# Attention layer with fp32-exact projections: ScalarE empties projection banks at the head of a unit, VectorE takes the softmax weight behind the score copy

## The reference

```python
def proj(w, b):
    return (x_seq @ w + b).reshape(B, S, NUM_HEADS, d_k).transpose(0, 2, 1, 3)
q, k, v = proj(wq, bq), proj(wk, bk), proj(wv, bv)
scores = jnp.einsum('bhqd,bhkd->bhqk', q, k) / jnp.sqrt(jnp.float32(d_k))
scores = scores + _spatial_bias_matrix(spatial_bias, H, W)[None, None]
attn = jax.nn.softmax(scores, axis=-1)
ctx = jnp.einsum('bhqk,bhkd->bhqd', attn, v).transpose(0, 2, 1, 3).reshape(B, S, d_model)
resid = ctx @ wo + bo + x_seq
out = (resid - mu) * jax.lax.rsqrt(var + LN_EPS) * ln_gamma + ln_beta
```

## Time and profile before

| | us |
|---|---|
| median of 3 runs | 4246.48 (4232.23 to 4246.49) |
| profiled execution | 4250.4 |
| its span, first to last instruction | 4248.5 |
| PE busy | 3415.7 (80%) |
| ACT busy | 2790.0 (66%) |
| DVE busy | 2606.1 (61%) |
| POOL busy | 1182.9 (28%) |
| granted PE clock, mean | 0.900 |

### The profile page before, as it was taken

How to read it: one execution, slowest core, us unless ns; L and a number is a source line. 1 busy time by engine, 2 the same in 40 slices (tenths; PEclk the granted TensorE clock), 3 DMA queues, 4 the chain that set the end, 5 groups by cost and what they waited for, 6 DMA issues and landing times. The chain is left out here.

```text
span 4248.5 us, 138744 instructions
## 1 busy us (share of the span) xinstructions
PE 3415.7 (80%) x52744; PEld 2233.4 (53%) x52744; DVE 2606.1 (61%) x5941; ACT 2790.0 (66%) x7015; POOL 1182.9 (28%) x2824
## 2 busy tenths in 40 slices
PE   4788788887888778888787887878888798877886
PEld 3455455554555455555555554545555555555554
DVE  2566666566666656656566565656656566666665
ACT  2676676766766667676666766667666676766764
POOL 0004214041240412315133150421404124041335
PEclk8899899898998989899898998989999899898988
DMA  4222222223222222312222222232222322222220
GB/s 136 54 62 59 70 64 65 56 61 75 57 64 56 69 61 59 78 46 67 65 57 72 54 60 65 57 76 57 66 55 63 73 57 65 55 68 67 58 64 19
DMA packets 318064, 269.31 MB, mean 63 GB/s; under 512 B 109883, under 2 KB 240955, under 8 KB 317271
## 3 DMA queue, kind: packets, MB, share of 16 engines
q10 hardware_dynamic: 145120, 129.00, 12.8%
q1 hardware_dynamic: 172152, 130.19, 12.1%
HBM read 193.73 MB, written 63.53 MB: 61 GB/s over the span
## 5 line engine op out<-in xcount | busy, mean ns | idle before, releaser
L791 ACT ACTIVATE prob<-prob,own 128x450 f32<-128x450 f32 x1920 | 1269.8, 663 | 1119.0 <-DVE own L922 1087.3
L922 DVE CUSTOM_DVE_ANT_0 prob<-s_ps,window 128x450 f32<-128x450 f32 x1920 | 1126.2, 624 | 694.1 <-PE s_ps L673 616.1
L807 ACT ACTIVATE prob<-prob,weight 128x450 f32<-128x450 f32 x1920 | 1169.6, 657 | 3.9 <-DVE weight L931 3.9
L941 DVE STREAM_TRANSPOSE prob_t<-prob 128x960 f32<-128x960 f32 x960 | 1126.2, 1173 | 52.8 <-ACT prob L807 31.9
L673 PE MATMUL s_ps<-k_sb,q_sb 64*32 64x450 f32 x15360 | 974.3, 613 | 177.6 <-DVE own L922 123.3
L588 PE MATMUL r_ps<-xt,w_sb 128*128 128x450 f32 x3072 | 771.1, 397 | 244.4 <-ACT q_sb L747 148.3
L693 PEld LDWEIGHTS pv_ps<-prob_t,values 64*64 64x64 f32 x30720 | 775.0, 137 | 245.4 <-issue 245.3
L693 PE MATMUL pv_ps<-prob_t,values 64*64 64x120 f32 x30720 | 830.3, 263 | 8.2 <-DVE prob_t L941 3.0
L588 PEld LDWEIGHTS r_ps<-xt,w_sb 128*128 128x128 f32 x3072 | 583.8, 199 | 425.1 <-ACT q_sb L747 155.1
L673 PEld LDWEIGHTS s_ps<-k_sb,q_sb 64*32 64x32 f32 x15360 | 245.8, 114 | 639.8 <-issue 637.9
L607 PE MATMUL r_ps<-wv_sb,xt 128*120 128x512 f32 (+1 forms) x1536 | 425.6, 429 | 181.6 <-DVE xt L906 109.9
(11 more groups left out here) (57 smaller groups left out, 1690.3 us busy)
## 6 DMA issues: line engine op xcount, KB each, us to landing
w_sb<-w_split ACTq DMA_DIRECT2D x126, 512.0 KB, 3.9
values<-v_dram ACTq DMA_DIRECT2D x256, 240.0 KB, 4.9
tokens<-in_x SPq DMA_DIRECT2D x214, 240.0 KB, 3.2
other<-own SPq DMA_DIRECT2D x1920, 1.0 KB, 1.7
out<-tokens SPq DMA_DIRECT2D x105, 240.0 KB, 2.7
v_dram<-stage SPq DMA_DIRECT2D x96, 240.0 KB, 2.6
v_dram<-stage SPq DMA_DIRECT2D x32, 180.0 KB, 2.1
tokens<-in_x SPq DMA_DIRECT2D x30, 120.0 KB, 2.4
```

The source lines that it names most:

```text
L791: nc.scalar.activation(prob[:, u % RING, head, 0:HALF], prob[:, u % RING, head, 0:HALF], ACT.Exp, scale=-1.0, bias=own[:, s, 0, c:c + 1], ...
L807: nc.scalar.activation(prob[:, u % RING, head, 0:HALF], prob[:, u % RING, head, 0:HALF], ACT.Copy, scale=weight[:, s, c:c + 1]).then_inc(p ...
L922: nc.vector.tensor_tensor_reduce(prob[:, u % RING, head, 0:HALF], s_ps[:, u % 2, head, 0:HALF], window[:, w0:w0 + HALF // GRID, :].rearran ...
L941: nc.vector.transpose(out=prob_t[:, g % 2, v % PER_GROUP, :, :].rearrange("p h k -> p (h k)"), in_=prob[:, u % RING, :, :].rearrange("p h ...
```

## The change

It is made in two of the five instruction streams, and moves instructions without adding or removing any. In ACT's `body` the loop over `im.evicted(u)` goes from the end of the unit to its head, ahead of the exponentials, the ratios, `normalise`, the loads of values and `keep_context`; the DMA that `keep_piece` issues goes with it. The units of `EVICT` stay, and so does the order of the evictions among each other. The evictions of the prologue (u < 0) keep their place. In DVE's `body`, `weights(u+2)` goes from ahead of `biased_scores(u+6)` to behind it. `PV_STEPS, FULL_STEPS` stay 2 and 8.

```diff
             def body(im, u):
+                for work in im.evicted(u):
+                    if work[0] == "xt":
+                        xt_hi(im, work[1])
+                    elif work[0] == "piece":
+                        keep_piece(im, *work[1:])
+                    elif work[0] == "value":
+                        stage_value(im, work[1])
                 if im.live(u + AHEAD):
                     exponentials(im, u + AHEAD)
                 if u % 2 and im.live(u + 3):
...
                 g = group_at(u - 1)
                 if g is not None:
                     keep_context(im, g)
-                for work in im.evicted(u):
-                    if work[0] == "xt":
-                        xt_hi(im, work[1])
-                    elif work[0] == "piece":
-                        keep_piece(im, *work[1:])
-                    elif work[0] == "value":
-                        stage_value(im, work[1])
 
             images(act, body)
...
             def body(im, u):
                 if im.live(u):
                     turn(im, u)
+                if im.live(u + AHEAD):
+                    biased_scores(im, u + AHEAD)
                 if u % 2 == 0 and im.live(u + 2):
                     weights(im, u + 2)
-                if im.live(u + AHEAD):
-                    biased_scores(im, u + AHEAD)
```

## The result

| | before | after |
|---|---|---|
| median, us | 4239.35 (4 runs, 4230.32 to 4246.49) | 3753.62 (4 runs, 3747.85 to 3760.88) |
| ratio | | 0.8856, 95% interval 0.8828 to 0.8884 |
| span of the profiled execution, us | 4248.5 | 3746.0 |
| granted PE clock | 0.900 | 0.949 |

What follows compares the result with a forecast made beforehand. Bound: a ring of waits, PE to DVE to ACT to bank to PE, no engine full. A 25.1 + B 9.8 + C 3.8 - D 1.3 = 37.4 us a turn, 579 in all: about 3667 us; forecast 3590 to 3780, range to 3970.

Steps and rivals of the forecast that it cites:

- C: DVE's weight behind the copy of the scores: the copy fills DVE's wait for POOL's total; 3.8 us a turn.
- A: ACT's evictions of pieces and values at the head: PE's stalls and the lower clock behind them go; 25.1 us an image.
- B: Input tiles evicted at ACT's head, batches 30 to 36: ACT sets the pace, 6.35 us a batch; 9.8 us won.
- D: New wait on ACT: value tile 7 at head of unit 54 waits for tile 5's store; costs 1.3 us.
- Rival 1: ACT and DVE set the pace once PE no longer stalls: 19 us won a turn, 3955 us; chance 0.25.
- Rival 4: ACT waits at the head for banks PE still fills, 4.4 us each at 14 odd-unit evictions: 4610 us; chance 0.07.
- Rivals 2 and 3: More goes than seen, under 3590 us, chance 0.08; another wait replaces PE's stall, 4246 us, chance 0.04.

Runs made afterwards that it cites:

- xt_tail: Changed kernel with input tiles and value tile 0 evicted at the end of ACT's unit as before: 3921.54 us, ratio 0.9256.
- act_only: Changed kernel with DVE's weight put back ahead of the copy, so only ACT's move is left: 3915.61 us, ratio 0.9234.
- pe_light: Changed kernel with one of the three products of each projection step left out on PE: 3720.18 us, ratio 0.878.
- act_load: Changed kernel with one more ACT copy of 128 columns in each unit, behind the exponentials: 3793.27 us, ratio 0.8956.
- dve_load: Changed kernel with one more DVE operation on 128 columns in each unit, behind the turn: 3754.94 us, ratio 0.8868.
- all_three: Changed kernel with SP's value stores and input-tile loads ahead of the exchange, and POOL's output bias ahead of scale and shift: 3645.16 us, ratio 0.8603.
- out_mid: all_three with DVE's sum of an output tile moved ahead of the copy of the scores: 3614.56 us, ratio 0.853.

## Why the prediction was right, and where not

**The direction and the mechanism** held. 3753.62 us lie inside the stated range, 87 us above the 3667 of the forecast and inside the forecast's own range (3590 to 3780). 486 us were won of 579. The first and the last image came as forecast in the profiled execution (32.3 and 23.4 us won, 32 and 23 said); what is short is the turn of the loop. That it is short by no more is in part luck, since errors of the terms cancel: C was worth more than I gave it, A without C less.

**A, evictions at the head.** The stalls for pieces and values went nearly as worked out, from 16.9 us an image to 2.1, where 0.2 was in the sum. The step that was short is that ACT comes to the head 4.4 us into the batch: in batch 26 it is 5.1 us, since ACT is still at the unit before. The stall of 5.05 us, for which I left 0.2, left 1.34; ahead of that eviction ACT's timeline has waits of 1.84 us for DVE's copy and 1.10 for POOL's `lead`. The stall of 2.76 left 0.61, and the one of 3.92 left 0.18.

**B, input tiles.** 9.8 us were forecast, `xt_tail` gives 11.2. Tiles 6 and 7 are evicted 1827.99 - 1804.27 = 23.7 us behind the exponentials of unit 36, where I said 22 and before it was 33.0 (the rows are of ACT's timeline):

```profile
1804.27 0.67 ACT L791 ACTIVATE prob<-prob,own 128x450 f32<-128x450 f32 x1 [0.46 <-DVE own L922]
...
1827.99 0.80 ACT L734 ACTIVATE xt<-r_ps 128x480 fp32r<-128x480 f32 x2
```

I had left 1.6 us of lower clock in, at the context of batch 34. It was gone; the values of batch 36 stayed slow:

```profile
1814.94 3.31 PE L693 MATMUL pv_ps<-prob_t,values 64*64 64x120 f32 x120
...
1823.74 1.01 PE L562 MATMUL r_ps<-ident,tokens 120*128 120x120 f32 x8 [1.32 <-DMA tokens<-in_x]
1829.69 8.26 PE L607 MATMUL r_ps<-wv_sb,xt 128*120 128x512 f32 x24 [4.95 <-DVE xt L906]
```

The context takes 3.31 us, full speed, in thirteen of the fourteen turns, where it took 4.7 to 4.9 in twelve of them before. The same transposes and a pair of scores stand ahead of it in both kernels; what differs are the waits among them, 1.57, 1.86 and 1.14 us in the turn of rows 5, 0.65 and 1.48 in this one. The 24 value matmuls behind 4.95 idle us take 8.26, where it was 7.28 behind 7.20 idle us; but over the turns both kernels lie between 7.2 and 8.6, so that is no difference. The Trainium skill's sentence that transposes don't release the gate (TensorE: Matmul & The Clock Gate, Part 4: PE-mode transpose) is neither borne out nor refuted by this; as I applied it, to the context, it was wrong.

The transfers of this stretch I had left out altogether. I followed ACT's, DVE's and PE's instructions and not the loads that SP issues behind the exchange: PE now waits 2.4 us a turn for tiles 5 to 7, a wait that had stood in the shade of the others.

**C, the weight.** The mechanism was right: DVE's wait went from 31.9 to 5.7 us a turn, ACT hardly waits for the weight (18.3 us in the whole execution, 3.9 before), and ACT's wait for the copy went from 1087.3 to 448.7 us with both moves (923.2 with this one alone). The size was wrong: 3.8 us a turn against 145 / 15 = 9.7 alone and 162 / 15 = 10.8 on top of ACT's move. The step that failed is "what I won already in A and B not counted". I had given A the whole stall in batch 26, of which 1.6 us were DVE's, and did the same in each place; what belonged to C stood under A. `act_only` shows it: without C, batch 26 takes 10.1 us and not 7.2, batch 18 12.1 and not 9.8 (means of fourteen turns). Batch 10 is the third place, 16.7 us without C and 14.0 with it, where I had given C the 1.1 us of idle time and nothing for the clock behind the stall. A by itself, without B and C, was not run.

**D, the new wait.** Named with its place and its length (some 4 us forecast on ACT, 4.6 to 4.9 measured), but taken at 1.3 where 2.7 is right, the upper bound. The slack that I saw at the scores of unit 64 was there: PE does them without a wait. But I did not follow the lag to the next unit. The copy of unit 63 comes late, and PE waits 1.42 us at the scores of 65; the rest is the lower clock of batch 58, which the sum had left out.

**Where the difference lies.** A turn was to win 37.4 us and won 31.9. By PE's timeline, from the first score matmul of one batch to that of the next, means of fourteen turns:

| batches | forecast, us | won, us |
|---|---|---|
| 0 to 4 | 4.3 | 2.2 |
| 6 to 28, with the output tiles | 18.3 | 16.9 |
| 30 to 36, input tiles | 9.8 | 8.8 |
| 38 to 56 | 6.3 | 6.2 |
| 58, the store | -1.3 | -2.2 |

In the first row PE stands 1.3 us a turn inside the context of batch 4, where it did not stand before and where the trace names no releaser; this was in no term. The second holds the late eviction in batch 18, the third the loads, the last D.

**The rivals.** Rival 1 was wrong as a time (3955) and half right as a mechanism. PE, DVE and ACT do close a ring: `pe_light` shows that PE's work over an image is no longer what sets the pace. But it is not closed by ACT's and DVE's amount of work, as I had it, and with that `act_load` and `dve_load` should have cost 150 us or more. Rival 4 did not come: ACT's waits for PE at L765 are 7.0 us a turn, 6.4 of them at value tile 0 where PE works meanwhile, and those at L747 and L734 0.4. Rivals 2 and 3 did not come.

## What to carry to other kernels

When an engine empties a buffer that another waits for, put the emptying at the head of its unit, and read from the trace when that engine arrives there and when the buffer is full: the gap of the two is the price. Then follow every queue that the moved step touches, the DMA issuer's too: the stores and loads behind it stay where they were (here they cost 46 and about 16 of 3754 us, and both were had by swapping two steps on SyncE). Where A, for which PE waits, itself waits for B, don't book the whole stall to A; a run of each part alone is what gives them their sizes.

## Not expected of the hardware

PE stands inside a context, for up to 2.5 us, with nothing that the trace shows it to wait for, 25 times in the changed kernel and twice before; the rows are of the waits of the whole execution and of one such place, where 14 of the 120 matmuls are left:

```profile
PE pv_ps L693 <- issue: 21.6, 25, 2.5
...
1709.30 0.64 PE L693 MATMUL pv_ps<-prob_t,values 64*64 64x120 f32 x14 [0.76 <-issue]
```

In `all_three` it is 30.8 us in 29 times and in `out_mid` 37.4 in 32. It grows as the kernel gets faster. It also has its place: in the changed kernel one of these stalls stands 18 to 23 us behind the start of each of the fourteen turns, in batch 4, and these make 17.8 of the 21.6 us. The cause was not tried. And the clock: 480 us less PE work, by the estimate above, made PE slower at the rest (0.949 to 0.914), so that some 167 of them came back as time at the lower clock.
